# Recurrent stage of a graph transformer: the layer norm's inverse deviation, its first and last iteration, and which engine starts a Newton chain

## What is computed

```python
def step(h, _):
    h = h + 0.01 * jnp.tanh(h)
    h = h * jax.nn.sigmoid(h)
    h = _layernorm(h, ln_w, ln_b)
    h = jnp.einsum('bsc,dc->bsd', h, W) + b
    return (h, None)
x, _ = jax.lax.scan(step, x, None, length=30)
...
x = x + _L1_ffn_ref(_layernorm(x, axis=-1), ln_w, ln_b, W, b)
```

## Time and profile before

| | |
|---|---|
| median of 3 runs | 3228.32 us |
| the profiled execution, its own time | 3229.77 us |
| its span, first to last instruction | 3228.0 us |
| granted TensorE clock, mean | 0.977 |
| TensorE busy | 3034.4 us, 94% |
| VectorE busy | 2831.7 us, 88% |
| ScalarE busy | 2382.6 us, 74% |
| GpSimd busy | 1722.1 us, 53% |

### The profile page before, as it was taken

How to read it: one execution, slowest core, us unless ns; L and a number is a source line. 1 busy time by engine, 2 the same in 40 slices (tenths; PEclk the granted TensorE clock), 3 DMA queues, 4 the chain that set the end, 5 groups by cost and what they waited for, 6 DMA issues and landing times. The chain is left out here.

```text
span 3228.0 us, 67245 instructions
## 1 busy us (share of the span) xinstructions
PE 3034.4 (94%) x16801; PEld 2092.0 (65%) x16801; DVE 2831.7 (88%) x8856; ACT 2382.6 (74%) x4988; POOL 1722.1 (53%) x1101
## 2 busy tenths in 40 slices
PE   6999896999999899999999489999999999999997
PEld 4666665888888577777777355555555555555556
DVE  4777776888888788888888779999999999999997
ACT  4666664444444577777777699999999999999993
POOL 2444444333332121211211058899898888888886
PEclk9999997999999999999999589999999999999999
DMA  4000000000000000000000035555555555555557
GB/s 130 17 19 16 16 16 14 1 0 0 0 0 0 25 14 10 13 12 11 13 10 4 3 132 195 198 184 188 198 190 184 197 195 184 190 199 188 187 197 245
DMA packets 135071, 290.03 MB, mean 90 GB/s; under 512 B 12081, under 2 KB 69601, under 8 KB 135009
## 3 DMA queue, kind: packets, MB, share of 16 engines
q1 hardware_dynamic: 118112, 280.89, 25.7%
q10 hardware_dynamic: 16896, 8.39, 0.9%
HBM read 278.88 MB, written 10.35 MB: 90 GB/s over the span
## 5 line engine op out<-in xcount | busy, mean ns | idle before, releaser
L1077 POOL TENSOR_TENSOR d_g<-d_g,d_rb 128x1024 f32<-128x1024 f32 x480 | 1121.1, 2371 | 269.6 <-DMA d_rb<-d_rstd_rows 269.6
L1265 PE MATMUL d_p_y<-d_g,d_w_main 128*128 128x512 f32 x1856 | 960.9, 599 | 0.0
L1279 PEld LDWEIGHTS d_p_gt<-ident,d_g 128*128 128x128 f32 x3840 | 466.0, 142 | 527.7 <-ACT d_g L1324 365.1
L1142 DVE BATCH_NORM_STATS2 d_stats<-d_p_gt 128x6 f32<-128x256 f32 x1920 | 712.7, 407 | 24.1 <-PE d_p_gt L1279 24.1
L1324 ACT ACTIVATE d_g<-d_th,d_bias 128x512 f32<-128x512 f32 x928 | 670.2, 722 | 67.1 <-DVE d_th L1135 37.3
L1135 DVE SCALAR_TENSOR_TENSOR d_th<-d_th,d_p_y 128x512 f32<-128x512 f32 x960 | 638.0, 665 | 4.4 <-ACT d_th L1320 4.3
L1320 ACT ACTIVATE d_th<-d_p_y,d_bias 128x512 f32<-128x512 f32 x928 | 621.7, 670 | 1.3 <-PE d_p_y L1265 1.2
L1279 PE MATMUL d_p_gt<-ident,d_g 128*128 128x128 f32 x3840 | 592.0, 277 | 0.0
L514 ACT ACTIVATE a_prob<-a_masked,a_neg_max 128x128 f32<-128x128 f32 x1024 | 327.4, 391 | 111.5 <-DVE a_neg_max L334 111.4
L434 PE MATMUL a_p_s<-a_k_heads,a_q_t 128*128 128x512 f32 x768 | 397.4, 599 | 0.5 <-DVE a_k_heads L310 0.5
L451 PEld LDWEIGHTS a_p_pv<-a_v_ones,a_prob_t 128*128 128x128 f32 x3072 | 373.7, 192 | 10.7 <-issue 10.3
(11 more groups left out here) (170 smaller groups left out, 4399.5 us busy)
## 6 DMA issues: line engine op xcount, KB each, us to landing
d_rb<-d_rstd_rows SPq DMA_DIRECT2D x480, 512.0 KB, 5.5
a_adj_in<-in_adj_dram SPq DMA_DIRECT2D x64, 256.0 KB, 2.8
out_dram<-d_out_sb ACTq DMA_DIRECT2D x32, 256.0 KB, 3.3
d_rstd_rows<-d_rstd_row SPq DMA_DIRECT2D x120, 16.0 KB, 1.4
m_w_sb<-in_L_ffn_w_dram SPq DMA_DIRECT2D x2, 512.0 KB
x_sb<-in_x_dram SPq DMA_DIRECT2D x1, 256.0 KB, 2.9
a_w_raw<-in_L_gnn_Wq_dram SPq DMA_DIRECT2D x2, 64.0 KB, 2.1
a_w_raw<-in_L_gnn_Wk_dram SPq DMA_DIRECT2D x2, 64.0 KB, 2.1
```

The costliest lines, as they stand in the source:

```text
L1077: nc.gpsimd.tensor_tensor(g[:, c, :], g[:, c, :], rb[:, buf, :], ALU.mult).then_inc(s_gs, 1)
L1142: ins = nc.vector.bn_stats(stats[:, q % 2, (j * CT + t) // 2].rearrange("p a s -> p (a s)"), p_gt[:, t * P:(t + 2) * P].rearrange("p (a c) ...
L1265: nc.tensor.matmul(p_y[:, c % 2, cols(u)], w_main[:], g[:, c, cols(u)], start=True, stop=True).then_inc(s_y, 1)
L1279: ins = nc.tensor.transpose(p_gt[:, t * P:(t + 1) * P], g[:, c, t * P:(t + 1) * P], ident[:])
```

## The change

Four edits to `recurrent_ffn`.

- Step 0 of the Newton chain leaves VectorE. ScalarE makes the sum plus P * EPS (`sum_squares`, an Identity activation of 128x32 from SBUF into the PSUM tile v, with a column of P * EPS as its bias), behind the copy of the row in the slot with c mod 4 = 2. `CHAIN` is 9; the chain starts in place 1 of that slot and waits for ScalarE's semaphore `s_v`. rstd has a buffer for each of the 4 groups, and the tiles v_x and work_x move to the PSUM bank of the transposed row.
- The normalisation of x in iteration 0 moves from ScalarE to GpSimd, as `tensor_scalar` (subtract the mean, multiply), for all 16 chunks ahead of the first scaling. The shift isn't made any more, and `XCHAIN` is 11.
- The last iteration's inverse deviation is not transposed, stored, spread or multiplied into g. `last_product` waits for silu alone, and `add_x` multiplies by the inverse deviation, four instructions of 128x128 a unit. `OUTS` is 8.
- TensorE transposes the row behind the first unit of the slot with c mod 4 = 2, no longer at the end of the one before.

```diff
-    CHAIN, XCHAIN, PLACES = 10, 12, 3
+    SPREADS = ALL_GROUPS - GROUPS
+    CHAIN, XCHAIN, PLACES = 9, 11, 3
...
-    OUTS = 4
+    OUTS = 8
...
-        rstd = sb("rstd", [P, GTILES])
+        rstd = sb("rstd", [P, GROUPS, GTILES])
...
-        v, work, v_x, work_x = (p_nw[:, n * GTILES:(n + 1) * GTILES] for n in range(4))
+        v, work = (p_nw[:, n * GTILES:(n + 1) * GTILES] for n in range(2))
+        v_x, work_x = (p_row[:, P + n * GTILES:P + (n + 1) * GTILES] for n in range(2))
...
             @block.gpsimd
...
+                def normalise_x(c, u):
+                    q = c // GC
+                    pool.wait_ge(s_xnw, (q + 1) * XCHAIN)
+                    for t in range(u * UT, (u + 1) * UT):
+                        n = c % GC * CT + t
+                        ins = nc.gpsimd.tensor_scalar(g[:, c, t * P:(t + 1) * P], x_sb[:, c * CT + t, :],
+                                                      stats_x[:, q, n // 2, n % 2, 1:2], rstd_x[:, q, n:n + 1],
+                                                      ALU.subtract, ALU.mult)
+                    ins.then_inc(s_xn, 1)
+
+                for c in range(CHUNKS):
+                    for u in range(UNITS):
+                        normalise_x(c, u)
+                pool.wait_ge(s_xn, CHUNKS * UNITS)
+                pool.wait_ge(s_prep, 10)
                 with pool.Fori(1, CHUNKS + 1) as i:
                     for c in range(CHUNKS):
                         scale(i, c)
-                    pool.wait_ge(s_prep, 10)
-                    pool.wait_ge(s_xn, CHUNKS * UNITS)
...
-                with pool.Fori(CHUNKS + 1, ITERS + 1) as i:
+                with pool.Fori(CHUNKS + 1, ITERS) as i:
                     for c in range(CHUNKS):
                         scale(i, c)
...
                 def newton(k, q, n):
-                    y = rstd[:]
+                    y = rstd[:, q, :]
                     if n == 0:
-                        dve.wait_ge(s_bn, units(GC * k + GC - 1, UNITS - 1))
-                        ins = nc.vector.tensor_scalar(v.rearrange("p (t a) -> p t a", a=2), stats[:, q % 2, :, :, 2],
-                                                      P * EPS, None, ALU.add)
+                        dve.wait_ge(s_v, k + 1)
+                        wait(dve, s_rt, k - GROUPS + 1)
+                        ins = nc.vector.tensor_scalar(y.bitcast(I32), v.bitcast(I32), -0.5, MAGIC, ALU.mult, ALU.add)
...
                 def newton_part(i, c, place):
                     k, q = GROUPS * i + (c - 6) // GC, (c - 6) // GC % GROUPS
-                    n = PLACES * ((c - 6) % GC) + place
-                    if n < CHAIN and live_group(k):
+                    n = PLACES * ((c - 6) % GC) + place - 1
+                    if 0 <= n < CHAIN and live_group(k):
                         newton(k, q, n)

                 def add_x(o, u):
-                    n = o * UNITS + u
+
+                    n, q = o * UNITS + u, o // GC
                     dve.wait_ge(s_y, units(SLOTS + o, u))
+                    dve.wait_ge(s_nw, CHAIN * (ALL_GROUPS - GROUPS + q + 1))
+                    dve.wait_ge(s_xb, CHUNKS)
                     wait(dve, s_out[n % OUTS], 16 * (n // OUTS))
...
+                    for t in range(UT):
+                        tile = u * UT + t
+                        ins = nc.vector.scalar_tensor_tensor(
+                            out=out_sb[:, n % OUTS, t * P:(t + 1) * P], in0=p_y[:, o % 2, tile * P:(tile + 1) * P],
+                            scalar=rstd[:, q, o % GC * CT + tile:o % GC * CT + tile + 1], in1=x_sb[:, o * CT + tile, :],
+                            op0=ALU.mult, op1=ALU.add)
+                    ins.then_inc(s_sum, 1)
...
                 def last_product(s, c, u):
-                    pe.wait_ge(s_gs, s - CHUNKS + 1)
+                    pe.wait_ge(s_g, units(s - CHUNKS, u))
...
-                def transpose_rstd(k):
+                def transpose_rstd(k, q):
                     pe.wait_ge(s_nw, CHAIN * (k + 1))
                     wait(pe, s_row, k)
-                    nc.tensor.transpose(p_rt, rstd[:], ident[:]).then_inc(s_rt, 1)
+
+                    pe.wait_ge(s_xnw, GROUPS * XCHAIN)
+                    nc.tensor.transpose(p_rt, rstd[:, q, :], ident[:]).then_inc(s_rt, 1)
...
-                        k = GROUPS * i + (c - 9) // GC
-                        if c % GC == 1 and live_group(k):
-                            transpose_rstd(k)
+                            k, q = GROUPS * i + (c - 10) // GC, (c - 10) // GC % GROUPS
+                            if c % GC == 2 and u == 0 and spread_group(k):
+                                transpose_rstd(k, q)
...
+                def sum_squares(k, q):
+                    act.wait_ge(s_bn, units(GC * k + GC - 1, UNITS - 1))
+                    wait(act, s_nw, CHAIN * k)
+                    nc.scalar.activation(v.rearrange("p (t a) -> p t a", a=2), stats[:, q % 2, :, :, 2],
+                                         ACT.Identity, bias=eps_col[:]).then_inc(s_v, 1)
...
                             nc.scalar.copy(rstd_row[:, q % 2, :], p_rt).then_inc(s_row, 1)
+                        k, q = GROUPS * i + (c - 6) // GC, (c - 6) // GC % GROUPS
+                        if c % GC == 2 and live_group(k):
+                            sum_squares(k, q)
                         if live(s):
                             tanh(s, c % 2, 1, col)
                             silu(s, c, 0, col)
-                        if first(i) and c + 1 < CHUNKS:
-                            normalise_x(c + 1, 0)
-                            normalise_x(c + 1, 1)
```

More of the change, by code:

```diff
@@ L969, in recurrent_ffn @@
         bias = sb("bias", [P, 1])
+        eps_col = sb("eps_col", [P, 1])
         b_col = sb("b_col", [P, 1])
@@ L1002, in recurrent_ffn @@
         s_bn = sem("stats_ready")
+        s_v = sem("sum_ready")
         s_nw = sem("newton_chain")
@@ L1027, in live_group, with spread_group @@
             return not isinstance(k, int) or 0 <= k < ALL_GROUPS
+        def spread_group(k):
+            return not isinstance(k, int) or 0 <= k < SPREADS
         def iterations(eng, body):
@@ L1032, in iterations @@
             body(1)
-            with eng.Fori(2, ITERS) as i:
+            with eng.Fori(2, ITERS - 1) as i:
                 body(i)
+            body(ITERS - 1)
             body(ITERS)
@@ L1062, in _ @@
                 body(0)
-                with sp.Fori(1, ITERS) as i:
+                with sp.Fori(1, ITERS - 1) as i:
                     body(i)
                 for par in range(2):
-                    sp.wait_ge(s_dw[par], 16 * ALL_GROUPS // 2)
+                    sp.wait_ge(s_dw[par], 16 * SPREADS // 2)
                     for j in range(GC):
-                        sp.wait_ge(s_rb[par * GC + j], 16 * ALL_GROUPS // 2)
+                        sp.wait_ge(s_rb[par * GC + j], 16 * SPREADS // 2)
             @block.gpsimd
@@ L1171, in newton @@
                         else:
-                            ins = nc.vector.scalar_tensor_tensor(out=y, in0=work, scalar=5.0 if n == 6 else 1.5, in1=y,
+                            ins = nc.vector.scalar_tensor_tensor(out=y, in0=work, scalar=5.0 if n == 5 else 1.5, in1=y,
                                                                  op0=ALU.add, op1=ALU.mult)
@@ L1211, in body @@
                             if c in (0, 1, 4, 5, 8, 9):
-                                for n in range(c % GC * 6, c % GC * 6 + 6):
+                                for n in range(c % GC * 6, min(c % GC * 6 + 6, XCHAIN)):
                                     newton_of_x(1 + c // GC, n)
@@ L1220, in _ @@
                     stats_of_x(GC + c)
-                    for n in range(3 * c, 3 * c + 3):
+                    for n in range(3 * c, min(3 * c + 3, XCHAIN)):
                         newton_of_x(0, n)
@@ L1236, in _ @@
                 link(nc.vector.tensor_copy(bias_bc[:], p_gt[:, P:2 * P]))
+                link(nc.vector.memset(eps_col[:], P * EPS))
                 iterations(dve, body)
-                dve.wait_ge(s_xb, CHUNKS)
                 add_x(CHUNKS - 1, 1)
@@ L1307, in _ @@
             def _(act):
-                def normalise_x(c, u):
-                    q = c // GC
-                    act.wait_ge(s_xnw, (q + 1) * XCHAIN)
-                    for t in range(u * UT, (u + 1) * UT):
-                        n = c % GC * CT + t
-                        ins = nc.scalar.activation(g[:, c, t * P:(t + 1) * P], x_sb[:, c * CT + t, :], ACT.Identity,
-                                                   bias=shift_x[:, q, n:n + 1], scale=rstd_x[:, q, n:n + 1])
-                    ins.then_inc(s_xn, 1)
                 def tanh(s, b, u, col):
@@ L1341, in body @@
                         k, q = GROUPS * i + (c - 10) // GC, (c - 10) // GC % GROUPS
-                        if c % GC == 2 and live_group(k):
+                        if c % GC == 2 and spread_group(k):
                             use = (GROUPS // 2) * (i + (c - 10) // GC // GROUPS) + q // 2
```

26 lines of the change are left out of this document (6 added, 20 removed).

## The result

The changed kernel took 3291.97 us (median of 4 runs, 3288.27 to 3293.45) against 3228.06 us before (4 runs): a ratio of 1.0193, with a 95% interval of 1.0181 to 1.0205. The forecast was 3251 us in 3225 to 3279. The sign was right, the size was not: +64 us instead of +23. The profiled execution took 3288.27 us, its span is 3286.4 us.

What follows compares the result with a forecast made beforehand. VectorE, never idle in the recurrent stage's middle, was taken as the bound, ScalarE as busiest in the first stretch. 52 - 20 - 9 = +23 us on the profiled 3229.8 gave 3253, or 3251 us against the median; range 3225 to 3279.

Steps and rivals of the forecast that it cites:

- What bounds the middle: Recurrent stage's 1284.00 us middle: VectorE is busy throughout, so time added to or taken from its order is kernel time.
- The wait that comes in: Middle: VectorE's first Newton step waits for ScalarE's sum_squares, queued behind silu and copy; net 0.45 us a group, 52 us.
- The Newton step's 0.095 us: Middle: one Newton step costs VectorE about 0.095 us, not its duration of 0.19; removing one gives 11 us.
- The normalisation on GpSimd: First stretch, iteration 0: moving the normalisation from ScalarE to GpSimd gains 20 us, within 10 to 27.6.
- Rival (D): First stretch: GpSimd bounds it at 0.8 us or more an instruction, gain gone, 3271 us; counted within the forecast's 0.78.
- The last iteration: Last stretch: transposes, stores, spreads and scalings go, add_x makes four smaller instructions for one; gain 9 us.
- The rest at zero: TensorE's later row transpose, one memset, x's Newton step and a peeled loop body: under 1 us together, taken as 0.
- (A): Middle: sum_squares is done when VectorE comes, so only the 0.095 us saving stays; -40 us, 3188 us; chance 0.08.
- (B): Whole kernel a wash: short sum_squares (37 us) with full gains at both ends; -2 us, 3226 us; chance 0.08.
- (C): Middle: the copy ahead of sum_squares waits for the moved transpose; each 0.3 us is 35 us more, 3286; chance 0.06.

Runs made afterwards that it cites:

- the experiment of the last iteration alone: The kernel before with only the edits of the last iteration, TensorE's transpose and the tiles' banks; 3222.36 us, ratio 0.9981.
- the kernel with repeated inputs: The changed kernel with sum_squares ahead of silu and GpSimd normalising 512 columns by two two-input instructions, mean or inverse deviation repeated; 3188.07 us, ratio 0.9877.

## Why the prediction was wrong

The step that failed is the term of the normalisation in the sum: -20 us, "10 to 27.6", where the first stretch grew by 11.3. That is 31 of the 41 us between forecast and result; the term of the wait gives 9, the others less than 1. In turn:

- **What bounds the middle** was right: VectorE without idle time, so that everything in its order counts. The middle has its new time from VectorE's first step alone.
- **The wait that comes in** was right in mechanism, place and count, and 14% short in size: 0.53 us a group (60.9 / 116) for a forecast of 0.45, inside its bounds. `sum_squares` took 0.29 us for an estimate of 0.32. The term that was mis-sized is the hand-over back to VectorE: 0.03 us was taken from the hand-over of VectorE to ScalarE, and the one from ScalarE to an idle VectorE is 0.13 us (2510.96 to 2511.09); `mix` then follows 0.13 behind where it was 0.09. In this group that makes 0.58 us, from 1.45 to 2.03; an average group lost a little less.
- **The Newton step's 0.095 us** was right: 0.094 by the experiment with `sum_squares` ahead of `silu`.
- **The normalisation on GpSimd** is the step that failed: a gain of 20 us, where the stretch grew by 11.3; with the normalisation back on ScalarE it is 8 us shorter with `sum_squares` on ScalarE and 10.6 without. The mechanism was named (what GpSimd's instruction takes), its size was wrong. The bounds of the instruction were 0.45 and 0.61 us, from a two-input multiply and from a `tensor_scalar` whose two scalars are constants. Both have no operand that is a column in SBUF, and the real one has two; it took 0.775. At 128 times 0.775 = 99 us GpSimd alone is longer than the whole stretch was with ScalarE. Rival (D) named this at 0.8 us, with the gain gone and 3271 us, but the prediction's own working would have given a loss: 128 times 0.8 us from 1801 end at 1903, and the scaling and the product behind it bring iteration 1 to 1909, 13 us later than 1895.40, for 3284 us in all. The rival closest to what happened was priced by zeroing a gain, and the range ended at a gain of 10.
- **The last iteration** was right: -9.2 for -9. VectorE sets its pace with four instructions of 128x128 a unit: it was busy 36.49 of the 36.55 us from the first `add_x` at 3246.98 to its end at 3283.53, and its last 88 instructions, 22 units, took 22.82 us.
- **The rest at zero** was right, by the experiment of the last iteration alone.
- **The rivals.** (A), the hidden wait, is what the middle does with `sum_squares` ahead of `silu`; its 3188 us needed the gain on GpSimd as well, and that the kernel with repeated inputs comes to 3188.07 is in part chance, for its terms are not those of (A). (B) and (C) did not happen. The point of decision of (B) was slightly off: with middle gains of 20 and 9 us it lies at 29 / 116 = 0.25 us a group and not at 0.27.
- The GPSIMD Engine Reference of the Trainium skill (Engine selection) has elementwise work with one input at roughly line rate on GpSimd. The trace disagrees for a small `tensor_scalar` with two columns: 0.775 us for 128 columns, where two of the very same form took VectorE 0.58 us together. The measurement decides, and the gain of 27.6 us by that page was not there.

The sum with the measured terms is 60.9 + 11.3 - 9.2 = 63 us, against 63.9 by the medians.

## What to carry to other kernels

Moving a small instruction off a saturated engine pays only if its result is there before that engine comes for it: look at what stands ahead of it in the other engine's queue, and whether that waits for the very engine one wants to relieve. Here the order of two calls was worth 71 us, while the instruction's own saving is 11. When an operation is new to an engine, price it by a row with the same kinds of operands; and when a range is bounded by "the gain", work out whether the new engine alone is longer than the old stretch.

## What was not expected of the hardware

- At the same 128 columns GpSimd's `tensor_scalar` took 0.58, 0.61 and 0.775 us with one operation and a column, two operations and no column, and two of each. VectorE takes 0.58 us for two of the last form.
- A `tensor_tensor` on GpSimd with 512 columns took 1.04 us when its second input repeats a value along 128 columns, against 1.27 with full inputs elsewhere in this program, so that two passes over a unit (2.12 us) beat four fused instructions (3.10 us).
- From the end of `sum_squares` on ScalarE to the start of an idle VectorE's step passed 0.13 us, and from the end of VectorE's `mix` to the start of ScalarE's `silu` 0.03 to 0.04.
- In iteration 0 of the changed kernel TensorE's granted clock was 0.50, its lower level of 1.2 GHz, for the whole stretch while it waited for GpSimd (busy 61.83 of 99.95 us), and 0.78 in the kernel with repeated inputs, where it was busy 47.09 of 69.58 us.
